# Late keys by values in the next chunk's step, and earlier copies of the keys and of xq

## What is computed

```python
x = layernorm(x)                                   # first norm; the residual adds the raw x
q = relu(q) + EPS; k = relu(k) + EPS               # per head, 64 wide
k_cumsum = jnp.cumsum(k, axis=2)
context = jnp.cumsum(jnp.einsum('bhnd,bhne->bhnde', k, v), axis=2)
D_inv = 1.0 / jnp.einsum('bhnd,bhnd->bhn', k_cumsum, q)
attn = jnp.einsum('bhnd,bhnde,bhn->bhne', q, context, D_inv)
x2 = x + attn @ Wo + bo
xn2 = layernorm(x2)
h = silu(fp4_linear(xn2, w_gate)) * fp4_linear(xn2, w_up)
out = x2 + fp4_linear(h, w_down)
```

## Time and profile before

| | us |
|---|---|
| median of 3 runs | 1724.25 (1718.62 to 1724.9) |
| profiled execution, device time | 1723.47 |
| its span in the profile | 1721.6 |
| PE busy | 1607.0 |
| PEld busy | 1509.5 |
| DVE busy | 1135.0 |
| ACT busy | 663.8 |
| POOL busy | 453.2 |

### The profile page before, as it was taken

The page is one execution under the profiler, slowest core; times in us unless marked ns, Lnnn a source line. Parts: engine busy times, 40 slices in busy tenths (PEclk is TensorE's granted clock), DMA queues, the critical chain, the costliest instruction groups (busy, mean ns, idle before and its releaser), DMA issues.

```text
span 1721.6 us, 55290 instructions
## 1 busy us (share of the span) xinstructions
PE 1607.0 (93%) x24484; PEld 1509.5 (88%) x24484; DVE 1135.0 (66%) x2439; ACT 663.8 (39%) x1272; POOL 453.2 (26%) x631
## 2 busy tenths in 40 slices
PE   7799999999999999999999999999999999999976
PEld 6789899888989989898988989989889988989965
DVE  8667666667666667666667656667666667666655
ACT  5343344333444333344333434333343333444322
POOL 3222232222232222233213232222232222232211
PEclk9899999999999999999999999999999999999988
DMA  4100000000000000000000000000000000000000
GB/s 139 38 3 14 9 11 14 11 15 15 14 5 14 11 14 15 14 5 14 14 12 14 14 5 14 12 14 15 14 5 14 11 14 14 14 5 14 6 11 10
DMA packets 22011, 26.80 MB, mean 16 GB/s; under 512 B 1808, under 2 KB 20752, under 8 KB 21776
## 3 DMA queue, kind: packets, MB, share of 16 engines
q1 hardware_dynamic: 21776, 23.27, 4.2%
HBM read 14.88 MB, written 8.39 MB: 14 GB/s over the span
## 4 chain that ended last, share of the span: by engine, by line
PE 78%; DVE 12%; ACT 4%; issue 4%; POOL 1%; DMA 1%; POOLq 0%; SPq 0%; ACTq 0%; DVEq 0%
PE bank L423 58%; PE bank L652 3%; PE bank L589 3%; PE bank L557 2%; PE bank L692 2%; PE bank L533 2%; DVE probs L1288 1%; DVE xT_lo L1148 1%; ACT xn L945 1%; PE bank L507 1%; ACT xT_hi L811 1%; PE bank L485 1%; PE bank L622 1%; POOL rstd L1094 1%; PE bank L642 1%
## 5 line engine op out<-in xcount | busy, mean ns | idle before, releaser
L1075 POOL TENSOR_SCALAR qkT<-qkT 128x512 f32<-128x512 f32 x256 | 187.5, 737 | 311.4 <-ACT qkT L805 311.1
L805 ACT ACTIVATE qkT<-bank 128x512 f32<-128x512 f32 x256 | 152.9, 598 | 289.6 <-PE bank L423 289.6
L423 PE MATMUL bank<-xT_hi,wqk_hi 128*128 128x256 f32 x1024 | 211.8, 288 | 0.6 <-DVE wu_lo L1148 0.6
L423 PE MATMUL bank<-xT_hi,wqk_lo 128*128 128x256 f32 x1024 | 203.4, 279 | 0.2 <-issue 0.2
L423 PE MATMUL bank<-xT_lo,wqk_hi 128*128 128x256 f32 x1024 | 203.2, 279 | 0.0
L1094 POOL TENSOR_TENSOR rstd<-var,minus_half 128x1 f32<-128x1 f32 x64 | 35.0, 548 | 526.7 <-DVE var L1353 526.7
L1148 DVE TENSOR_TENSOR hqT_lo<-bank,hqT_hi 128x512 fp32r<-128x512 f32 (+1 forms) x128 | 68.9, 555 | 141.4 <-ACT hqT_hi L929 138.0
L423 PEld LDWEIGHTS bank<-xT_hi,wqk_hi 128*128 128x128 f32 x1024 | 155.4, 188 | 3.0 <-DVE wu_lo L1148 0.8
L423 PEld LDWEIGHTS bank<-xT_hi,wqk_lo 128*128 128x128 f32 x1024 | 156.2, 188 | 0.4 <-issue 0.4
L423 PEld LDWEIGHTS bank<-xT_lo,wqk_hi 128*128 128x128 f32 x1024 | 156.1, 188 | 0.0
L1148 DVE TENSOR_TENSOR attnT_lo<-bank,attnT_hi 128x512 fp32r<-128x512 f32 x128 | 88.4, 691 | 68.5 <-ACT attnT_hi L923 68.5
(11 more groups left out here) (172 smaller groups left out, 3999.7 us busy)
## 6 DMA issues: line engine op xcount, KB each, us to landing
x_in<-in_L_attn_x SPq DMA_DIRECT2D x32, 256.0 KB, 2.8
out<-out_sb SPq DMA_DIRECT2D x64, 128.0 KB, 1.7
qkT<-in_L_attn_Wq SPq DMA_DIRECT2D x1, 1024.0 KB, 8.1
qkT<-in_L_attn_Wk SPq DMA_DIRECT2D x1, 1024.0 KB, 10.2
probs<-in_L_attn_Wv SPq DMA_DIRECT2D x1, 512.0 KB, 4.0
k_tok<-in_L_attn_Wv SPq DMA_DIRECT2D x1, 512.0 KB, 6.0
attn<-in_L_attn_Wo SPq DMA_DIRECT2D x1, 512.0 KB, 11.4
x<-in_L_attn_Wo SPq DMA_DIRECT2D x1, 512.0 KB, 12.4
```

What stands on the lines that cost most here:

```text
L423: at = pe.matmul(dst, lhs_at(kt), rhs_at(kt), start=first and kt == 0, stop=last and kt == k_tiles - 1)
L805: act.activation(flat(qkT[:, 2 * m:2 * m + 2, :]), bank[bank_of["qk", c, n]][:], ACT.Relu).then_inc(qk_relu, 1)
L1075: pool.tensor_scalar(at, at, QK_EPS, 1.0, ALU.add, ALU.mult).then_inc(qk_ready, 1)
```

## The change

Three things are done. First, the late keys by values of chunk c - 1 leave the end of attend and stand ahead of the scores in the step of chunk c (late_keys, for c = 1, 2, 3). They no longer add to the early product in its bank: they get two banks of their own (late_kv), and VectorE adds them to state_mid instead (add_late, from state_mid and the bank to state), ahead of the first mask of the step; add_state behind normalize is gone. The kv banks are now free at state_mid_ready. The spare places leave the table, which gives many later writes another bank. Second, ScalarE copies k_tok and the high part of xq ahead of xn2. Third, VectorE makes the low part of xq ahead of the rounding (begin_x) instead of between its two halves. The count of instructions is the same on every engine.

```diff
+            keys += [("late_kv", c, n) for n in range(2) if c]
             keys += [("x", c, 0)] * (not odd) + [("scores", c, n) for n in range(2 if update else 4)]
...
-            held = [("spare", c, n) for n in range(2) if update]
             for n in range(2):
-                keys += [("qk", c, 2 * n), ("qk", c, 2 * n + 1)] * odd + held * (odd and not n) + [("hq", c, n)]
-            keys += held * (not odd)
+                keys += [("qk", c, 2 * n), ("qk", c, 2 * n + 1)] * odd + [("hq", c, n)]
...
+            def keys_by_values(c, kv, late):
+
+                for j in range(HALF_PAIRS):
+                    for n in range(2):
+                        pair = j + HALF_PAIRS * n
+                        rows = key_rows(pair, late)
+                        for odd in range(2):
+                            at = pair * P + DH * odd
+                            last = pe.matmul(bank[kv[n]][DH * odd:DH * odd + DH, j * VW:(j + 1) * VW],
+                                             k_tok[rows, at:at + DH], v1[c // 2][rows, c % 2, 2 * pair + odd, :],
+                                             start=j == 0, stop=True, skip_group_check=True)
+                return last
+
+            def late_keys(b, c):
+
+                kv = [banks.take(pe, ("late_kv", c, n), b, state_ready, lambda b: (CHUNKS - 1) * b + c)
+                      for n in range(2)]
+                keys_by_values(c - 1, kv, True).then_inc(kv_done, 1)
...
-                kv = [banks.take(pe, ("kv", c, n), b, state_ready, lambda b: (CHUNKS - 1) * b + c + 1)
+                kv = [banks.take(pe, ("kv", c, n), b, state_mid_ready, lambda b: (CHUNKS - 1) * b + c + 1)
                       for n in range(2)]
...
-                for j in range(HALF_PAIRS):
-                    for n in range(2):
-                        for odd in range(2):
-                            last = keys_by_values(kv[n], j + HALF_PAIRS * n, odd, True)
-                last.then_inc(kv_done, 1)
...
                 if now:
+                    if c:
+                        late_keys(b, c)
                     if c < CHUNKS - 1:
                         scores(b, c, g, u)
...
-                if normed:
-                    act.wait_ge(ln2_shift, g)
-                    act.activation(xn2[:], x2[:, (c - 1) % CHUNKS, :], ACT.Identity, bias=shift2[:],
-                                   scale=rstd2[:]).then_inc(xn2_ready, 1)
                 if now and c < CHUNKS - 1:
...
                 if gated and not last:
                     high_xq()
+                if normed:
+                    act.wait_ge(ln2_shift, g)
+                    act.activation(xn2[:], x2[:, (c - 1) % CHUNKS, :], ACT.Identity, bias=shift2[:],
+                                   scale=rstd2[:]).then_inc(xn2_ready, 1)
...
+                def add_late():
+
+                    got = side_by_side("late_kv", c, 0)
+                    held, mid = (t.rearrange("p (n j) e -> p n (j e)", n=2) for t in (state[:], state_mid))
+                    dve.wait_ge(state_mid_ready, (CHUNKS - 1) * b + c)
+                    dve.wait_ge(kv_done, (CHUNKS - 1) * b + c)
+                    dve.tensor_tensor(held, mid, got, ALU.add).then_inc(state_ready, 1)
...
+                if now and c:
+                    add_late()
...
+                if gated and not last:
+                    low_xq()
                 if normed:
                     begin_x()
...
-                if gated and not last:
-                    low_xq()
...
-                if now and c < CHUNKS - 1:
-                    add_state()
```

More of the change, by code:

```diff
@@ L242, in build_program @@
         for key in keys:
-            if key[0] in ("av", "kv") and key[2] % 2 == 0 and len(spread) % 8 == 7:
+            if key[0] in ("av", "kv", "late_kv") and key[2] % 2 == 0 and len(spread) % 8 == 7:
                 spread.append(("none", len(spread), 0))
@@ L312, in build_program @@
         W_BANKS = [("hq", 0, 0), ("hq", 0, 1), ("gate_up", 0, 2), ("xq", 1, 0), ("gate_up", 1, 0), ("gate_up", 1, 2),
[L313 removed]
+                   ("hq", 2, 0), ("hq", 2, 1), ("hq", 2, 0), ("hq", 2, 1)]
         def ffn_turns(job):
@@ L528, in attend @@
                 v = v1[c // 2]
-                def keys_by_values(k, pair, odd, late):
-                    rows = key_rows(pair, late)
-                    j, at = pair % HALF_PAIRS, pair * P + DH * odd
-                    return pe.matmul(bank[k][DH * odd:DH * odd + DH, j * VW:(j + 1) * VW], k_tok[rows, at:at + DH],
-                                     v[rows, c % 2, 2 * pair + odd, :], start=not late and j == 0, stop=late,
-                                     skip_group_check=True)
                 pe.wait_ge(k_ready, 2 * ((CHUNKS - 1) * b + c + 1))
-                kv = [banks.take(pe, ("kv", c, n), b, state_ready, lambda b: (CHUNKS - 1) * b + c + 1)
+                kv = [banks.take(pe, ("kv", c, n), b, state_mid_ready, lambda b: (CHUNKS - 1) * b + c + 1)
                       for n in range(2)]
-                for j in range(HALF_PAIRS):
-                    for n in range(2):
-                        for odd in range(2):
-                            last = keys_by_values(kv[n], j + HALF_PAIRS * n, odd, False)
-                last.then_inc(kv_early_done, 1)
+                keys_by_values(c, kv, False).then_inc(kv_early_done, 1)
                 to = [[banks.take(pe, ("av", c, 2 * half + odd), b, attn_ready,
```

9 lines of the change are left out of this document (removed).

## The result

| | before | after |
|---|---|---|
| median, us | 1724.58 (1718.62 to 1726.69) | 1670.26 (1669.79 to 1675.0) |
| profiled execution, device time | 1723.47 | 1669.97 |
| its span | 1721.6 | 1668.2 |
| TensorE's issue gaps, all lines | 28.3 | 4.9 |
| wait of the hq transposes for the state | 13.2 | 0 |

The last four rows are sums over the profiled execution, the issue gaps with the few at other lines. The direction was right and the sum was not.

What follows compares the result with a forecast made beforehand. TensorE sets the time, busy 1607.0 of 1721.6 us, so its idle 114.6 us could be gained. Terms -15.7 - 10.3 - 1.0 + 0.5 = -26.5 us gave 1697.5 us, range 1690 to 1703 (chance 0.58).

Steps and rivals of the forecast that it cites:

- the early copies: ScalarE's and VectorE's copies of keys and xq: they fit into idle time, cost nothing there and gain nothing.
- The wait of the hq transposes: Third steps: 14 TensorE waits for VectorE's addition to the state, in a shared bank, go; 15.7 us saved, bounds 10 to 16.
- The issue gaps by the shorter run: Late keys leave attend's dense run, so two thirds of 15.4 us of gaps there go: 10.3 saved, bounds 0 to 18.
- The end: Last sequence's third step: attend's 2.69 us wait for the residual goes, partly given back; 1 us saved, 0 to 3.
- VectorE's chain: Head of the step: add_late delays VectorE's chain by 0.60 us, TensorE comes 0.58 later; 0.5 us lost in total.
- Those in queries by state at 10 to 13: Sign: issue gaps in attend's queries by state stay at 10 to 13 us, from 11.8 before.
- The waits for the values at 0.8: Sign: attend's waits for ScalarE's copy of the values stay at 0.8 us, 15 times.
- The wait for state_mid at 0.5: Sign: the wait for state_mid grows from 0.18 to some 0.5 us, while that for xqT_lo goes.
- PE busy within 5 us: Sign: TensorE's busy time stays the same within 5 us.
- hq for GpSimd in fourth steps: Sign of being wrong: a new wait of hq for GpSimd; 0.2 to 0.3 of 0.48 us cover expected used.
- More goes than I count: Rival: all 15.4 of gaps and 3 more, 16 for hq, 3 for the end, 4 at the scores; 1683, chance 0.12.
- The gaps only move: Rival: instruction transfers take as long and TensorE runs dry elsewhere, so no gap saving; 1708 us, chance 0.17.

Runs made afterwards that it cites:

- copies alone: The kernel before with only ScalarE's and VectorE's new orders: keys and xq copied ahead of xn2, low xq ahead of the rounding; 1703.91 us, ratio 0.9892.
- move alone: The changed kernel with ScalarE's and VectorE's old orders put back, keeping the late keys' new place, their own banks and the new table; 1688.61 us, ratio 0.9804.
- the keys' copies by themselves: The changed kernel with only the two k_tok copies ahead of xn2, both parts of xq made where they were before; 1671.85 us, ratio 0.9707.
- one wait put back ahead of attend: The changed kernel with one added TensorE wait, for VectorE's x_inv_ready, at attend's first group, copies still early; 1684.54 us, ratio 0.9786.
- the run with that bank alone: The kernel before with two third-step bank entries changed: second hq bank on 7, first gate_up bank entry on 5; 1708.51 us, ratio 0.9917.
- the run with the copies and the hq bank: The kernel before with the new ScalarE and VectorE orders and the two changed bank entries, late keys still ending attend; 1685.7 us, ratio 0.978.

## Why the prediction was wrong, point by point

**The step that failed** is the one on the early copies: "They gain nothing either." It priced them by attend's wait for xqT_lo and by what is late behind that, and there it was right: in the run with the copies alone that time comes back at the values and state_mid. It had no term for TensorE's short wait for the keys ahead of attend's first group (the 0.72 us that became 0.56), and did not ask whether the place of such a wait matters to the transfers of instructions. It had named the gaps as such, from the earlier trace rows, and let only the length of the dense run act on them. The runs showed a second cause: copies alone -19.1 us, with 17.5 us less of gaps; from the move alone to after -18; the keys' copies by themselves enough; one wait put back ahead of attend, 13 us slower. The forecast's 1697.5 less these 18 is 1679.5, already below its range.

**The second thing missed** is the first sequence, 7.5 us faster, where nothing was predicted; 5.6 of them are in its first two steps. Part of it is the granted clock of TensorE. This is the same stretch of its work in the first step, from the second transposes of hq to the last product with Wo, before and after (columns as above):

```profile
41.30:51.79 10.49, 7.29 (x37) 6.71 (x38) 6.43 (x11) 2.31 (x4) 3.09 (x2) 0.67 0.14 44
```

```profile
40.80:46.87 6.07, 4.47 (x36) 4.27 (x37) 5.93 (x10) 1.57 (x3) 2.75 (x2) 1.00 0.27 78
```

It took 4.4 us less, of which 1.3 are paid back behind it, for the late keys at their new place and a wait of 0.64. Both had a wait of 1.26 us at the start of the stretch. Then TensorE waited for the low part of a weight:

```profile
44.81 0.45 PE L652 MATMUL bank<-ident,attn 128*128 128x128 f32 x1 [2.42 <-DVE wg_lo L1148]
```

```profile
43.92 1.19 PE L421 MATMUL bank<-wo_hi,attnT_hi 128*128 128x256 f32 x8 [1.60 <-DVE wg_lo L1149]
```

Before, the granted clock was at 1.2 GHz from 44.8 to 51.6, right behind this wait; after, it stayed at 2.4 GHz. It was down once more before, from 96.0 to 99.4, behind the wait for the keys of 1.69 us at 94.12 and one of 0.83 for the values. After, the first of these is gone, a wait of 1.12 us of the value products for the state has come at 86.78, that for the values is 1.28, and the clock did not fall. Over the first 140 us the clock was at 1.2 GHz for 17 us before and 7 after (mean 0.94 and 0.98), so at most some 5 us of matmul time. The runs without the move took 109.5 to 110.3 us for the first sequence, move alone and after 105.8 and 104.1, so most of it comes with the move. That the shorter wait is what kept the clock up was not tested.

**The terms of the sum.**
- *The wait of the hq transposes, 15.7*: right, 14.5 by the run with that bank alone. Nothing was late behind it.
- *The issue gaps by the shorter run, 10.3*: right in size and in its reason. The gaps behind edges in attend's second group went from 13.9 to 2.6 us with the move alone (those behind edges in its first group grew from 9.3 to 12.1), and from 9.8 to 0.8 from the run with the copies and the hq bank to after. In time the move gave 9.1 us in the middle sequences on top of the hq bank (102.2 to 101.55 each, 14 of them) and 8.7 on top of hq bank and copies. One of the twelve gaps that the term was made from was no gap of instructions but the wait for the keys at 94.12.
- *The end, 1.0*: 1.7 measured. The wait of 2.7 for the residual is gone.
- *VectorE's chain, +0.5*: not to be told apart. A wait of the values for the state has appeared once, 1.1 us in the first sequence; in the middle sequences there is none.

Together: 38.4 for the hq bank and the copies, where one by one they gave 14.5 and 19.1; then 8.7 for the move's gaps, 6.3 in the first sequence and 1.8 at the end, less 1.2 at the start. That makes 54.0 of the 54. Why the first two together give 5 more than one by one isn't settled; it is about what the intervals leave open.

**The signs.** No wait of hq for the state: so. 0.63 us from hq to gate: so. Gaps in keys by values at a few us: none. Those in queries by state at 10 to 13: wrong, 2.7; they are 16.2 in the run with the move alone. The waits for the values at 0.8: wrong, 1.3 (17.2 us in all), because TensorE comes to them sooner by what it no longer waits for ahead of attend. The wait for state_mid at 0.5: it is 0.8, for the same reason. A new wait of the values for the state, one of the signs of being wrong: once. PE busy within 5 us: wrong, 20.7 less, for the gaps and waits that its groups had held within. hq for GpSimd in fourth steps: no new wait, as said.

**The rule that was weighed.** By the Trainium skill (Runtime: NRT & Kernel Launch, section Instruction fetch mechanics) the fetch of instructions hides behind their issue, and the term for the gaps would have been 0. The runs are against that here: 27 gaps with 26.7 us before, each at a 256th record, gone to 4.9 without one matmul less. The 256 instructions of the same section are borne out by that count.

**The rivals.** "More goes than I count" was nearest in outcome, 1683, but by another mechanism. "The gaps only move" is refuted: they don't keep their number (27 to 4), although the transfers do.

**What stays open**: why a wait ahead of attend's first group holds the transfer back, while at edges in the second group it starts 0.4 to 1.8 us behind with waits there (0.4 for xqT_lo, 1.3 for the values) as without. The runs tell the place, not the reason.

## What to carry to other kernels

A wait that is covered by a later one was not free here, where a long run of short instructions followed it: it delayed the transfer of the next instructions. So where such a run shows issue gaps, try the copies that it needs at the front of their engine's queue, even when the engine chain behind is not helped, and try the run shorter: here each acted on gaps that the other left. A test that adds instructions moves the edges too, so count the gaps by their edges before you read it. And where a bank table deals banks in turn, read for each wait which earlier tenant of the bank it stands for: two entries (hq, gate) gave 14.5 us here, and two more (the values) with one moved addition 34.4.

## What the runs showed of the hardware

- TensorE ran dry at some of its block edges, every 256th of its records, where they pass at about 8 ns each (64 in 0.52 us, so 256 in 2.1 to 3.1 us with waits): 27 of some 195 edges before, 26.7 us in all. A gap of 0.2 to 1.8 us ended 2.2 to 2.9 us after the start of a transfer of 16.4 KB.
- When the transfer starts isn't fixed to that count. At edges in attend's first group it started 0.5 to 2.4 us behind the edge in 10 of 11 cases before, and 0.1 to 1.3 us ahead of it in 9 of 12 with the copies early. With them the gaps were 15.9 us fewer (26.7 to 10.8).
- At edges in the second group it started 0.5 to 1.8 us behind in the runs with the late keys in attend, and 0.4 to 1.7 in those without; by the table 46 of 106 and 8 of 118 of these edges were followed by a gap.
- A wait of 0.2 to 0.3 us, hidden by the next one, made the kernel 13 us slower through this.
- The granted clock was at 1.2 GHz for some 17 us of the first 140 before and some 7 after, with the same work in other order.
